# Loading the adjacency matrix through GpSimd's DMA path with a type conversion, in a graph layer with residual and layer norm

## The chip, the cores and the metric

One core of a Trainium2 chip. The metric is the time of one execution on the device in microseconds; lower is better. All inputs and the output lie in the chip's memory in float32, adj in int32.

## What is computed

x is 8 x 2048 x 512, adj is 2048 x 2048 of zeros and ones (int32), W is 512 x 1024.

```python
Wi, Wj = W[:, :512], W[:, 512:]
mi = einsum('bkd,od->bko', x, Wi)
mj = einsum('bkd,od->bko', x, Wj)
a = adj.astype(float32)
deg = a.sum(axis=1)
y = x + deg[None, :, None] * (mi + b) + einsum('ij,bjo->bio', a, mj)
out = (y - mean(y)) / sqrt(var(y) + 1e-5)      # over the last axis
```

The kernel receives x also as tiles transposed for TensorE (xt), and adj transposed and cut into 64 chunks: adjt[q, j] holds 128 rows j of the transposed matrix by 512 columns q, 256 KB in int32.

## The kernel before

**Stages.** The program runs batch 0, then a loop over batches 1 to 6, then batch 7. A batch has 16 tiles of 128 nodes. First the projections: for each tile n, TensorE makes mj and mi, each as a cross product (L343, 4 matmuls) and a main product (L351 and L353, 8 matmuls). Then the aggregations: for each tile i, 32 matmuls (L375) of the widened adjacency columns adjT with all of mj_hi and mj_lo of the batch. Numbers are split into a part of high bits and a rest so that TensorE's products keep float32 precision; hence x_top, x_hi, x_lo, x_df for x, and mj_hi, mj_lo for mj.

**Start.** Tiles 0 and 1 of batch 0 are projected straight from float32 weights (project_native), while VectorE and ScalarE split the 8 weight chunks (split_w L555 to L561, copy_w_hi L425). w_top, a scratch of that splitting, lies in the upper half of adjT8's columns.

**One projected tile, engine by engine.** Every engine has its own instruction stream, worked off in order, and waits on semaphores.
- VectorE (L665 to L681): mj(n) from PSUM (L587); the split of x(n+2) into x_top (L576) and the rest (L579), which waits for x_df(n+1), since x_top is one buffer (L575); mi(n) from PSUM (L594).
- ScalarE (L493 to L513): x_hi(n+1) and x_lo(n+1) (L443, L445), the copies of the cross products (L454), the load of x_raw(n+3), mj_hi(n) (L458).
- GpSimd (L300 to L307): x_df(n+1) (L281) after x_lo(n+1), then mj_lo(n) (L286) after mj_hi(n).
- TensorE (L380 to L392): the two halves of tile n, h = 0 after x_df(n) (L337).
- SP (L221 to L232): stores mi(n) to a buffer in the chip's memory.

**One aggregated tile.** ScalarE widens 128 columns of adjT8, from int8 to float32, into adjT (L470; two buffers). GpSimd adds the bias to mi read back (add_bias, L292). VectorE makes the residual with deg (L622), then, when TensorE is done, the sum and the layer norm (L628 to L649). agg_ps has two buffers.

**The adjacency, in batch 0 alone.** SP loads a chunk c as int32 into one of AB = 4 staging buffers adj_in (L176); ScalarE casts it to int8 into its place in adjT8 (cast_chunk, L465); VectorE adds the same int32 buffer into deg_part, the running sum of 16 chunks (count_chunk, L605 for the first of 16, L608 for the others). A buffer is loaded again when cast and count are both done (L174, L175). From deg_part TensorE makes the degrees (L360) once for each of four column blocks. Two lists written out by hand set the order, two chunks for each projected tile from tile 2 and up to four for each aggregated tile:

```python
PROJ_CHUNKS = [0, 0, 2, 2, 2, 2, 2, 2, 2, 2, 2, 2, 2, 2, 2, 2]
AGG_CHUNKS = [2, 3, 3, 3, 3, 3, 3, 4, 4, 4, 4, 0, 0, 0, 0, 0]
```

In a projected tile the first chunk is counted after the split of x(n+2), the second after mi(n). SP issues the loads of the chunks at matching places between its stores. The staging buffers 2 and 3 hold, before that, the first two tiles of x (x_first, L91).

Of the kernel before, what the change touches and what calls it, by code (L numbers as in the profile page):

```python
# [5 lines left out]
def bass_adj_resnorm(nc, x, xt, adjt, wt, b, out):  # L6
    fp32 = mybir.dt.float32
    fp32r = mybir.dt.float32r
    bf16 = mybir.dt.bfloat16
    i32 = mybir.dt.int32  # L10
    u32 = mybir.dt.uint32
    i8 = mybir.dt.int8
    ALU = mybir.AluOpType
# [8 lines left out]
    IB = N // DO  # L22
    TPB = DO // P
    GT = 4
    AB = 4
    NG = NT // GT
    NP = NT // 2
    TILES = NB * NT
# [11 lines left out]
    with ctx:  # L40
# [25 lines left out]
        mi = sb("mi", [P, DO], fp32)  # L66
        mi_in = [sb(f"mi_in{s}", [P, DO], fp32) for s in range(2)]
        r = [sb(f"r{s}", [P, D], fp32) for s in range(GT)]
        adj_in = [sb(f"adj_in{s}", [P, DO], i32) for s in range(AB)]
        deg_part = [sb(f"deg_part{s}", [P, DO], fp32r) for s in range(2)]  # L70
        bias = sb("bias", [P, DO], fp32)
        deg = sb("deg", [P, NT], fp32)
# [15 lines left out]
        w_stage = [r[0], r[1], r[2], r[3], mi_in[0], mi_in[1], x_top, mi]  # L88
        scratch = [adjT8[:, 2 * q:2 * q + 2, N // 2:N].bitcast(fp32) for q in range(NT // 2)]
        w_top = scratch  # L90
        x_first = [adj_in[2][:, :].bitcast(fp32), adj_in[3][:, :].bitcast(fp32)]  # L91

        def halves(ap):
            return ap.rearrange("p (a d) -> p a d", a=2)
# [21 lines left out]
        mi_loaded = [sem(f"mi_loaded{s}") for s in range(2)]  # L116
        r_loaded = [sem(f"r_loaded{s}") for s in range(GT)]
        adj_loaded = [sem(f"adj_loaded{s}") for s in range(AB)]
        adj_cast = sem("adj_cast")
        deg_part_ready = sem("deg_part_ready")  # L120
        deg_in_psum = sem("deg_in_psum")
        deg_ready = sem("deg_ready")
# [46 lines left out]

        @block.sync  # L170
        def _(sp):
            def load_chunk(c):
                if c >= AB:
                    sp.wait_ge(adj_cast, c - AB + 1)  # L174
                    sp.wait_ge(deg_part_ready, c - AB + 1)  # L175
                sp.dma_start(adj_in[c % AB][:, :], adjt[c // NT, c % NT]).then_inc(adj_loaded[c % AB], 16)  # L176

            def store_mi(n):
                sp.wait_ge(mi_ready, n + 1)
                sp.dma_start(mi_dram[n], mi[:, :]).then_inc(mi_stored, 16)  # L180

            sp.dma_start(x_first[0], xt[0]).then_inc(x_first_loaded[0], 16)
            for c in range(DK + 1, 2 * DK):
                sp.dma_start(w_stage[c][:, :], wt[c]).then_inc(w_loaded[c], 16)
            sp.dma_start(x_first[1], xt[1]).then_inc(x_first_loaded[1], 16)
            for c in range(DK):
                sp.dma_start(w_stage[c][:, :], wt[c]).then_inc(w_loaded[c], 16)
            for s in range(2):
                sp.dma_start(x_raw[s][:, :], xt[NATIVE + s]).then_inc(x_loaded[s], 16)
            sp.dma_start(bias[:, :], b.partition_broadcast(P)).then_inc(b_loaded, 16)  # L190
            for c in range(2):
                load_chunk(c)
            for n in range(NATIVE):
                sp.wait_ge(main_done, NATIVE + n + 1)
                load_chunk(2 + n)
                store_mi(n)

            def load_mi(m, u):
# [5 lines left out]
            def batch(bt):  # L204
                zero = known(bt) and bt == 0
                final = known(bt) and bt == NB - 1
                base = NT * bt

                def first_loads():
                    if zero:  # L210
                        sp.wait_ge(w_ready, 2 * DK)
                        sp.wait_ge(main_done, 2 * NATIVE)
                    sp.wait_ge(mi_stored, 16 * (base + 2))
                    for u in range(2):
                        load_mi(base + u, u)
                    for u in range(GT - 1):
                        if not zero:
                            sp.wait_ge(out_stored[u], 16 * NG * bt)
                        load_r(base + u, u)

                def proj(g):  # L221
                    for u in range(GT):
                        if zero and GT * g + u < NATIVE:
                            continue
                        if zero:
                            for c in proj_chunks(GT * g + u)[:-1]:
                                load_chunk(c + AB)
                        store_mi(base + GT * g + u)
                        if zero:
                            load_chunk(proj_chunks(GT * g + u)[-1] + AB)  # L230
                        if known(g) and g == NG - 1 and u == 1:
                            first_loads()  # L232

                over_groups(sp, zero, True, proj)

                def agg(g):
                    for u in range(GT):
                        i = GT * g + u
                        m = base + i
                        begin = known(g) and g == 0  # L240
                        ending = known(g) and g == NG - 1
                        if begin and u == 0:
                            sp.wait_ge(mi_stored, 16 * (base + NT))
                        if not (ending and u >= GT - 2):
                            sp.wait_ge(res_ready, m + 1)
                            load_mi(m + 2, u)
                        if not (ending and u >= 1):
                            if not (zero and begin and u == 0):
                                sp.wait_ge(out_stored[(u + 3) % GT], 16 * (NG * bt + g + (u + 3) // GT))
                            load_r(m + 3, (u + 3) % GT)  # L250
                        if zero:
                            for c in agg_chunks(i):
                                if c + AB < CHUNKS:
                                    load_chunk(c + AB)
                        sp.wait_ge(norm_ready, m + 1)
                        if final and ending and u == GT - 1:
                            sp.dma_start(out_tiles[m, :, 0:DO // 2], r[u][:, 0:DO // 2]).then_inc(out_stored[u], 16)
                        else:
                            sp.dma_start(out_tiles[m], r[u][:, :]).then_inc(out_stored[u], 16)

                agg(0)
                if zero:
                    for g in range(1, NG - 1):
                        agg(g)
                else:
                    with sp.Fori(1, NG - 1) as g:
                        agg(g)
                agg(NG - 1)
# [6 lines left out]
        def _(pool):  # L275
# [14 lines left out]
            def add_bias(m, u, turn):  # L290
                pool.wait_ge(mi_loaded[u % 2], turn)
                pool.tensor_tensor(mi_in[u % 2][:, :], mi_in[u % 2][:, :], bias[:, :], ALU.add).then_inc(mib_ready, 1)  # L292

            difference(NATIVE, 0)

            def batch(bt):
                zero = known(bt) and bt == 0
# [2 lines left out]
                def proj(g):  # L300
                    for u in range(GT):
# [3 lines left out]
                        if not (final and known(g) and g == NG - 1 and u == GT - 1):  # L305
                            difference(n + 1, (u + 1) % 2)
                        rest_of_mj(n, GT * g + u)  # L307

                over_groups(pool, zero, final, proj)
                if zero:  # L310
                    pool.wait_ge(b_loaded, 16)
                with pool.Fori(0, NP) as k:
                    for u in range(2):
                        add_bias(NT * bt + 2 * k + u, u, 16 * (NP * bt + k + 1))

            over_batches(pool, batch)

# [104 lines left out]
        def _(act):  # L422
# [35 lines left out]
                nc.scalar.activation(mj_hi[:, bass.ds(t, 1), :].rearrange("p t d -> p (t d)"), mj[:, :],  # L458
                                     ACT.Copy).then_inc(mj_hi_ready, 1)

            def cast_chunk(c):
                s = c % AB
                act.wait_ge(adj_loaded[s], 16 * (c // AB + 1))
                q, j = c // NT, c % NT
                nc.scalar.activation(adjT8[:, j, q * DO:(q + 1) * DO], adj_in[s][:, :], ACT.Copy).then_inc(adj_cast, 1)  # L465

            def widen(i, s, chunks):
                if chunks is not None:
                    act.wait_ge(adj_cast, chunks)
                nc.scalar.activation(adjT[s][:, :, :], adjT8[:, :, bass.ds(i * P, P)], ACT.Copy).then_inc(adjT_ready, 1)  # L470

            def root(m):
# [16 lines left out]
            def batch(bt):  # L489
# [3 lines left out]
                def proj(g):  # L493
                    last_group = known(g) and g == NG - 1
                    for u in range(GT):
# [6 lines left out]
                        take_cross(n, 0)  # L502
                        if not (final and last_group and u >= GT - 3):
                            load_x(n + 3, (u + 1) % 2)
                        if zero:
                            for c in proj_chunks(t)[:-1]:
                                cast_chunk(c)
                        take_cross(n, 1)
                        top_of_mj(n, t)
                        if zero:  # L510
                            cast_chunk(proj_chunks(t)[-1])
                        if last_group and u in (0, 2):
                            widen(u // 2, u // 2, NT if zero else None)  # L513

# [7 lines left out]
                    proj(NG - 1)  # L522
                if zero:
                    for i in range(NT):
                        for c in agg_chunks(i):
                            cast_chunk(c)
                        if i < NT - 2:
                            act.wait_ge(agg_done, i + 1)
                            widen(i + 2, i % 2, NT * ((i + 2) // TPB + 1))
                        if i == NT - 1:  # L530
                            parts(NT + 1, 1)
                        root(i)
# [18 lines left out]
        def _(dve):  # L551
# [43 lines left out]
                                               ALU.mult, ALU.subtract).then_inc(mi_ready, 1)  # L595

            def count_chunk(c):
                s = c % AB
                dve.wait_ge(adj_loaded[s], 16 * (c // AB + 1))
                q = c // NT  # L600
                part = deg_part[q % 2]
                if c % NT == 0:
                    if q >= 2:
                        dve.wait_ge(deg_in_psum, q - 1)
                    nc.vector.tensor_copy(part[:, :], adj_in[s][:, :]).then_inc(deg_part_ready, 1)  # L605
                else:
                    dve.wait_ge(deg_part_ready, c)
                    nc.vector.tensor_tensor(part[:, :], part[:, :].bitcast(fp32), adj_in[s][:, :],  # L608
                                            ALU.add).then_inc(deg_part_ready, 1)

            def take_degrees(q):
# [133 lines left out]
```

## Time and profile before

| | us |
|---|---|
| median of 3 runs | 1643.63 (1643.55 to 1643.64) |
| the profiled execution, whole | 1643.72 |
| its span | 1641.9 |
| TensorE busy | 1634.2 |
| VectorE busy | 844.8 |
| ScalarE busy | 661.7 |
| GpSimd busy | 498.4 |

The page gives the busy time of each engine (PE is TensorE's matmuls, PEld its weight loads, DVE is VectorE, ACT ScalarE, POOL GpSimd) and the chain that ended last, followed back from the end. The timeline gives start, duration and engine, and behind "<-" what ended an engine's idle time. TensorE's clock was granted at 0.999 of full speed.

### The profile page before, as it was taken

The numbers are of one execution on the slowest core, as the hardware profiler recorded it, in microseconds if no ns is written. First come the engines' busy times: TensorE is split into PE (matmuls) and PEld (weight loads), VectorE is DVE, ScalarE is ACT, GpSimd is POOL, SyncE is SP. The second block draws the span as 40 slices with busy tenths as digits, with TensorE's granted clock in tenths as the row PEclk, the third lists the DMA queues.
The fourth block names the chain that finished last, engine by engine and source line by source line (L and its number), as shares of the span: only waits on it lengthen the run. The fifth ranks groups of instructions, "written<-read, shape, count | busy, mean of one in ns | idle before, by whom it ended". The sixth has DMA issues, their size and how long they took to land.

```text
span 1641.9 us, 24654 instructions
## 1 busy us (share of the span) xinstructions
PE 1634.2 (100%) x7196; PEld 1346.8 (82%) x7196; DVE 844.8 (51%) x1879; ACT 661.7 (40%) x964; POOL 498.4 (30%) x386
## 2 busy tenths in 40 slices
PE   9999999999999999999999999999999999999998
PEld 6888888888888888888888888888888888888886
DVE  8787644554444544444544544444544454544544
ACT  5765445332453324532245332452325522255221
POOL 3532134311343114431144211442114421144210
PEclk9999999999999999999999999999999999999999
DMA  6676422332234323243223332233323333233332
GB/s 205 193 226 223 141 84 94 131 108 96 83 102 133 100 93 96 89 134 109 84 95 101 123 115 83 95 114 117 102 83 102 124 106 106 74 101 115 96 115 70
DMA packets 102843, 187.27 MB, mean 114 GB/s; under 512 B 11424, under 2 KB 11680, under 8 KB 102816
## 3 DMA queue, kind: packets, MB, share of 16 engines
q1 hardware_dynamic: 84672, 154.05, 29.1%
q10 hardware_dynamic: 18144, 32.91, 6.3%
q8 instruction: 11, 0.18, 0.0%
q14 instruction: 16, 0.13, 0.0%
HBM read 119.80 MB, written 67.11 MB: 114 GB/s over the span
## 4 chain that ended last, share of the span: by engine, by line
PE 98%; DVE 1%; DMA 0%; issue 0%; POOL 0%; ACT 0%; DVEq 0%
PE agg_ps L375 57%; PE cross_ps L343 14%; PE main_ps L351 14%; PE main_ps L353 14%; DVE W_lo L558 0%; DVE W_df L561 0%; DMA mi_in<-in_wt 0%; DVE adjT L555 0%; DVE x_raw L579 0%; DVE mj_lo L568 0%; PE deg_ps L360 0%; POOL x_df L281 0%; DVE x_top L576 0%; DVE stats L630 0%; DVE r L628 0%
## 5 line engine op out<-in xcount | busy, mean ns | idle before, releaser
L375 PE MATMUL agg_ps<-mj_hi,adjT 128*128 128x512 f32 x2048 | 797.0, 389 | 0.0
L375 PE MATMUL agg_ps<-mj_lo,adjT 128*128 128x512 f32 x2048 | 796.7, 389 | 0.0
L470 ACT ACTIVATE adjT<-adjT 128x2048 fp32r (+1 forms) x128 | 245.4, 1917 | 562.8 <-PE agg_ps L375 562.8
L375 PEld LDWEIGHTS agg_ps<-mj_hi,adjT 128*128 128x128 f32 x2048 | 384.5, 188 | 79.9
L375 PEld LDWEIGHTS agg_ps<-mj_lo,adjT 128*128 128x128 f32 x2048 | 384.3, 188 | 79.7
L351 PE MATMUL main_ps<-W_hi,x_hi 128*128 128x512 f32 x1008 | 392.3, 389 | 0.0
L353 PE MATMUL main_ps<-W_lo,x_lo 128*128 128x512 f32 x1008 | 392.1, 389 | 0.0
L292 POOL TENSOR_TENSOR mi_in<-mi_in,bias 128x512 f32<-128x512 f32 x128 | 166.9, 1307 | 649.9 <-DMA mi_in<-mi_dram 649.9
L628 DVE TENSOR_TENSOR r<-agg_ps,r 128x512 f32<-128x512 f32 x128 | 88.6, 692 | 355.0 <-PE agg_ps L375 354.9
L343 PE MATMUL cross_ps<-W_df,x_df 128*128 128x512 f32 x1008 | 270.2, 390 | 0.6 <-DVE W_df L561 0.5
L286 POOL TENSOR_TENSOR mj_lo<-mj,mj_hi 128x512 f32 (+1 forms) x126 | 166.7, 1323 | 323.4 <-ACT mj_hi L458 323.4
L454 ACT ACTIVATE cross<-cross_ps 128x512 f32<-128x512 f32 x252 | 148.6, 590 | 215.0 <-PE cross_ps L343 213.5
L343 PEld LDWEIGHTS cross_ps<-W_df,x_df 128*128 128x128 f32 x1008 | 189.0, 188 | 40.9 <-DVE W_df L561 0.9
L351 PEld LDWEIGHTS main_ps<-W_hi,x_hi 128*128 128x128 f32 x1008 | 189.3, 188 | 39.8 <-DVE mi L594 0.3
L353 PEld LDWEIGHTS main_ps<-W_lo,x_lo 128*128 128x128 f32 x1008 | 189.1, 188 | 39.2
L281 POOL TENSOR_TENSOR x_df<-x_top,x_lo 128x512 fp32r<-128x512 f32 x126 | 164.9, 1309 | 150.1 <-ACT x_lo L445 149.8
L587 DVE SCALAR_TENSOR_TENSOR mj<-main_ps,cross 128x512 f32<-128x512 f32 x126 | 87.1, 691 | 224.0 <-PE main_ps L353 218.8
L594 DVE SCALAR_TENSOR_TENSOR mi<-main_ps,cross 128x512 f32<-128x512 f32 x126 | 87.0, 691 | 107.6 <-PE main_ps L353 105.7
L622 DVE SCALAR_TENSOR_TENSOR r<-mi_in,deg,r 128x512 f32<-128x512 f32 x128 | 101.4, 796 | 13.1 <-POOL mi_in L292 9.2
L443 ACT ACTIVATE x_hi<-x_top 128x512 fp32r<-128x512 f32 x126 | 79.6, 632 | 63.3 <-PE main_ps L353 61.3
L630 DVE BATCH_NORM_STATS2 stats<-r 128x6 f32<-128x512 f32 x128 | 89.0, 695 | 11.7
L579 DVE TENSOR_TENSOR x_raw<-x_raw,x_top 128x512 f32<-128x512 f32 x126 | 87.3, 693 | 4.3
(59 smaller groups left out, 592.1 us busy)
## 6 DMA issues: line engine op xcount, KB each, us to landing
mi_dram<-mi SPq DMA_DIRECT2D x128, 256.0 KB, 2.1
mi_in<-mi_dram SPq DMA_DIRECT2D x128, 256.0 KB, 2.7
r<-in_x SPq DMA_DIRECT2D x128, 256.0 KB, 2.6
out<-r SPq DMA_DIRECT2D x127, 256.0 KB, 2.1
x_raw<-in_xt ACTq DMA_DIRECT2D x124, 256.0 KB, 2.7
adj_in<-in_adjt SPq DMA_DIRECT2D x64, 256.0 KB, 3.9
r<-in_wt SPq DMA_DIRECT2D x4, 256.0 KB, 5.2
adj_in<-in_xt SPq DMA_DIRECT2D x2, 256.0 KB, 4.0
```

The lines of the kernel that those rows point to most:

```text
L281: pool.tensor_tensor(x_df[s][:, :], x_top[:, :], x_lo[s][:, :].bitcast(fp32), ALU.subtract).then_inc(x_df_ready, 1)
L286: pool.tensor_tensor(mj_lo[:, bass.ds(t, 1), :].rearrange("p t d -> p (t d)"), mj[:, :], mj_hi[:, bass.ds(t, 1), :].rearrange("p t d -> p ...
L292: pool.tensor_tensor(mi_in[u % 2][:, :], mi_in[u % 2][:, :], bias[:, :], ALU.add).then_inc(mib_ready, 1)
L343: last = nc.tensor.matmul(cross_ps[h][:, :], x_df[s][:, k * P:(k + 1) * P], W_df[:, half * DK + k, :], start=(k == 0), stop=(k == DK - 1))
L351: nc.tensor.matmul(main_ps[h][:, :], x_hi[s][:, k * P:(k + 1) * P], W_hi[:, half * DK + k, :], start=(k == 0), stop=False)
L353: last = nc.tensor.matmul(main_ps[h][:, :], x_lo[s][:, k * P:(k + 1) * P], W_lo[:, half * DK + k, :], start=False, stop=(k == DK - 1))
L375: last = nc.tensor.matmul(agg_ps[s][:, :], adjT[s][:, j, :], part[:, j, :], start=(j == 0 and part is mj_hi), stop=(j == NT - 1 and part i ...
L454: nc.scalar.activation(cross[h][:, :], cross_ps[h][:, :], ACT.Copy).then_inc(cross_ready, 1)
L470: nc.scalar.activation(adjT[s][:, :, :], adjT8[:, :, bass.ds(i * P, P)], ACT.Copy).then_inc(adjT_ready, 1)
L622: nc.vector.scalar_tensor_tensor(r[u][:, :], mi_in[u % 2][:, :], deg[:, bass.ds(i, 1)], r[u][:, :], ALU.mult, ALU.add).then_inc(res_ready, 1)
L628: nc.vector.tensor_tensor(r[u][:, :], agg_ps[s][:, :], r[u][:, :], ALU.add).then_inc(sum_ready, 1)
L630: nc.vector.bn_stats(stats[:, :], r[u][:, :]).then_inc(ln_step, 1)
```

## The change

The chunks are loaded by GpSimd's DMA path, with int32 made int8 by the transfer, straight into adjT8. The casts on ScalarE and the staging buffers go; counting reads adjT8's int8. The number of chunks in flight, AB, goes from 4 to 8; a chunk c is issued when count c - 8 is done. Chunks 0 and 1 are issued before x_df of tile 2, chunks 2 to 7 directly behind it. In batch 0's projections chunks c + 8 follow mj_lo(n) in GpSimd's stream; in its aggregation they follow add_bias of the next tile, in a loop now written out. Chunk 32 also waits for the weights to be split. x_first gets two buffers of its own.

```diff
-    AB = 4
+    AB = 8
-        adj_in = [sb(f"adj_in{s}", [P, DO], i32) for s in range(AB)]
+        x_first = [sb(f"x_first{s}", [P, D], fp32) for s in range(2)]
...
         @block.sync
-            def load_chunk(c):
-                if c >= AB:
-                    sp.wait_ge(adj_cast, c - AB + 1)
-                    sp.wait_ge(deg_part_ready, c - AB + 1)
-                sp.dma_start(adj_in[c % AB][:, :], adjt[c // NT, c % NT]).then_inc(adj_loaded[c % AB], 16)
...
-            for c in range(2):
-                load_chunk(c)
             for n in range(NATIVE):
-                sp.wait_ge(main_done, NATIVE + n + 1)
-                load_chunk(2 + n)
                 store_mi(n)
...
         @block.gpsimd
+            def load_chunk(c):
+                q, j = c // NT, c % NT
+                if c >= AB:
+                    pool.wait_ge(deg_part_ready, c - AB + 1)
+                if q == 2 and j == 0:
+                    pool.wait_ge(w_ready, 2 * DK)
+                    pool.wait_ge(w_hi_ready, 2 * DK)
+                pool.dma_start(adjT8[:, j, q * DO:(q + 1) * DO], adjt[q, j]).then_inc(adj_loaded[c % AB], 16)
+
+            for c in range(2):
+                load_chunk(c)
             difference(NATIVE, 0)
+            for c in range(2, AB):
+                load_chunk(c)
...
                         rest_of_mj(n, GT * g + u)
+                        if zero:
+                            for c in proj_chunks(GT * g + u):
+                                load_chunk(c + AB)
...
+                if zero:
+                    for i in range(NT):
+                        add_bias(i, i % 2, 16 * (i // 2 + 1))
+                        if i:
+                            for c in agg_chunks(i - 1):
+                                if c + AB < CHUNKS:
+                                    load_chunk(c + AB)
...
         @block.scalar
-            def cast_chunk(c):
-                s = c % AB
-                act.wait_ge(adj_loaded[s], 16 * (c // AB + 1))
-                q, j = c // NT, c % NT
-                nc.scalar.activation(adjT8[:, j, q * DO:(q + 1) * DO], adj_in[s][:, :], ACT.Copy).then_inc(adj_cast, 1)
-
             def widen(i, s, chunks):
                 if chunks is not None:
-                    act.wait_ge(adj_cast, chunks)
+                    act.wait_ge(deg_part_ready, chunks)
...
         @block.vector
             def count_chunk(c):
-                s = c % AB
-                dve.wait_ge(adj_loaded[s], 16 * (c // AB + 1))
-                q = c // NT
-                part = deg_part[q % 2]
-                if c % NT == 0:
+                dve.wait_ge(adj_loaded[c % AB], 16 * (c // AB + 1))
+                q, j = c // NT, c % NT
+                part, chunk = deg_part[q % 2], adjT8[:, j, q * DO:(q + 1) * DO]
+                if j == 0:
                     if q >= 2:
                         dve.wait_ge(deg_in_psum, q - 1)
-                    nc.vector.tensor_copy(part[:, :], adj_in[s][:, :]).then_inc(deg_part_ready, 1)
+                    nc.vector.tensor_copy(part[:, :], chunk).then_inc(deg_part_ready, 1)
                 else:
                     dve.wait_ge(deg_part_ready, c)
-                    nc.vector.tensor_tensor(part[:, :], part[:, :].bitcast(fp32), adj_in[s][:, :],
+                    nc.vector.tensor_tensor(part[:, :], part[:, :].bitcast(fp32), chunk,
                                             ALU.add).then_inc(deg_part_ready, 1)
```

The calls of load_chunk on SP and of cast_chunk on ScalarE in batch 0's tiles go too.

## Rows read from the trace of the kernel before

**Rows 1.** The page: busy time and share of the span; chain that ended last.

```profile
PE 1634.2 (100%) x7196; PEld 1346.8 (82%) x7196; DVE 844.8 (51%) x1879; ACT 661.7 (40%) x964; POOL 498.4 (30%) x386
PE 98%; DVE 1%; DMA 0%; issue 0%; POOL 0%; ACT 0%; DVEq 0%
```

**Rows 2.** Busy time by stretch, the projections of batch 0; then clock, DMA share, GB/s.

```profile
25.00:97.00 72.00, 72.00 (x319) 59.45 (x320) 57.37 (x82) 54.14 (x96) 38.42 (x27) 1.00 0.65 200
```

**Rows 3.** Timeline, TensorE: tiles 3, 4 and 15, and aggregation (start us, us).

```profile
24.95 1.20 PE L343 MATMUL cross_ps<-W_df,x_df 128*128 128x512 f32 x4
30.52 1.07 PE L343 MATMUL cross_ps<-W_df,x_df 128*128 128x512 f32 x4
...
91.02 1.07 PE L343 MATMUL cross_ps<-W_df,x_df 128*128 128x512 f32 x4
96.46 0.39 PE L375 MATMUL agg_ps<-mj_hi,adjT 128*128 128x512 f32 x1
```

**Rows 4.** Groups of instructions, 0 to 160 us, ScalarE's casts of the chunks.

```profile
L465 ACT ACTIVATE adjT<-adj_in 128x512 int8<-128x512 int32 x55 | 33.8, 625 | 6.8 <-DMA adj_in<-in_adjt 6.7
```

**Rows 5.** Timeline: an issue on SP, and GpSimd's instruction at its longest.

```profile
17.15 0.34 SPq L180 DMA_DIRECT2D mi_dram<-mi  x1
...
46.57 1.75 POOL L286 TENSOR_TENSOR mj_lo<-mj,mj_hi 128x512 fp32r<-128x512 f32 x1 [2.22 <-ACT mj_hi L458]
```

**Rows 6.** Timeline, the start: first weight, VectorE's start, GpSimd's gap and VectorE's instruction in it.

```profile
0.75 0.42 ACTq L476 DMA_DIRECT2D mi_in<-in_wt  x1
4.15 0.43 DVE L555 TENSOR_SCALAR adjT<-mi_in 128x512 uint32<-128x512 uint32 x1 [4.15 <-DMA mi_in<-in_wt]
16.20 1.45 POOL L281 TENSOR_TENSOR x_df<-x_top,x_lo 128x512 fp32r<-128x512 f32 x1 [15.21 <-ACT x_lo L445]
18.12 0.42 DVE L555 TENSOR_SCALAR adjT<-r 128x512 uint32<-128x512 uint32 x1
23.60 1.29 POOL L281 TENSOR_TENSOR x_df<-x_top,x_lo 128x512 fp32r<-128x512 f32 x1 [5.95 <-ACT x_lo L445]
```

**Rows 7.** DMA: GB/s in 40 slices of 0 to 220 us; KB and us to landing.

```profile
GB/s 204 399 121 182 95 192 194 194 237 199 219 201 202 172 180 122 275 339 207 161 252 238 214 203 216 219 206 240 243 225 235 279 77 143 103 97 43 48 49 95
...
adj_in<-in_adjt SPq DMA_DIRECT2D x64, 256.0 KB, 3.9
```

**Rows 8.** Timeline, GpSimd and VectorE: split, count, mi and count of projected tiles.

```profile
51.91 0.69 DVE L608 TENSOR_TENSOR deg_part<-deg_part,adj_in 128x512 fp32r<-128x512 f32 x1
52.63 0.69 DVE L594 SCALAR_TENSOR_TENSOR mi<-main_ps,cross 128x512 f32<-128x512 f32 x1
53.24 1.06 DVE L608 TENSOR_TENSOR deg_part<-deg_part,adj_in 128x512 fp32r<-128x512 f32 x1
...
93.96 1.30 POOL L281 TENSOR_TENSOR x_df<-x_top,x_lo 128x512 fp32r<-128x512 f32 x1 [2.00 <-ACT x_lo L445]
95.39 0.43 DVE L576 TENSOR_SCALAR x_top<-x_raw 128x512 uint32<-128x512 uint32 x1 [0.24 <-POOL x_df L281]
95.85 0.69 DVE L579 TENSOR_TENSOR x_raw<-x_raw,x_top 128x512 f32<-128x512 f32 x1
96.46 1.78 DVE L608 TENSOR_TENSOR deg_part<-deg_part,adj_in 128x512 fp32r<-128x512 f32 x1
```

**Rows 9.** Timeline, GpSimd and VectorE: the first chunks counted, beside an x_df.

```profile
26.10 1.52 DVE L605 CAST deg_part<-adj_in 128x512 fp32r<-128x512 int32 x1
27.30 1.47 POOL L281 TENSOR_TENSOR x_df<-x_top,x_lo 128x512 fp32r<-128x512 f32 x1
28.14 1.18 DVE L608 TENSOR_TENSOR deg_part<-deg_part,adj_in 128x512 fp32r<-128x512 f32 x1
```

**Rows 10.** Timeline, aggregation of batch 0: idle before add_bias and the sum; four counts.

```profile
140.34 1.30 POOL L292 TENSOR_TENSOR mi_in<-mi_in,bias 128x512 f32<-128x512 f32 x1 [6.04 <-DMA mi_in<-mi_dram]
140.75 0.69 DVE L628 TENSOR_TENSOR r<-agg_ps,r 128x512 f32<-128x512 f32 x1 [0.80 <-PE agg_ps L375]
159.27 3.08 DVE L608 TENSOR_TENSOR deg_part<-deg_part,adj_in 128x512 fp32r<-128x512 f32 x4
```

More of the change, by code:

```diff
@@ L9, in bass_adj_resnorm @@
     bf16 = mybir.dt.bfloat16
-    i32 = mybir.dt.int32
     u32 = mybir.dt.uint32
@@ L90, in bass_adj_resnorm @@
         w_top = scratch
-        x_first = [adj_in[2][:, :].bitcast(fp32), adj_in[3][:, :].bitcast(fp32)]
         def halves(ap):
@@ L118, in bass_adj_resnorm @@
         adj_loaded = [sem(f"adj_loaded{s}") for s in range(AB)]
-        adj_cast = sem("adj_cast")
         deg_part_ready = sem("deg_part_ready")
@@ L180, in store_mi @@
                 sp.dma_start(mi_dram[n], mi[:, :]).then_inc(mi_stored, 16)
-            sp.dma_start(x_first[0], xt[0]).then_inc(x_first_loaded[0], 16)
+            sp.dma_start(x_first[0][:, :], xt[0]).then_inc(x_first_loaded[0], 16)
             for c in range(DK + 1, 2 * DK):
                 sp.dma_start(w_stage[c][:, :], wt[c]).then_inc(w_loaded[c], 16)
-            sp.dma_start(x_first[1], xt[1]).then_inc(x_first_loaded[1], 16)
+            sp.dma_start(x_first[1][:, :], xt[1]).then_inc(x_first_loaded[1], 16)
             for c in range(DK):
@@ L224, in proj @@
                             continue
-                        if zero:
-                            for c in proj_chunks(GT * g + u)[:-1]:
-                                load_chunk(c + AB)
                         store_mi(base + GT * g + u)
-                        if zero:
-                            load_chunk(proj_chunks(GT * g + u)[-1] + AB)
                         if known(g) and g == NG - 1 and u == 1:
@@ L250, in agg @@
                             load_r(m + 3, (u + 3) % GT)
[L251 to L254, printed above, removed]
                         sp.wait_ge(norm_ready, m + 1)
@@ L311, in batch @@
                     pool.wait_ge(b_loaded, 16)
-                with pool.Fori(0, NP) as k:
-                    for u in range(2):
-                        add_bias(NT * bt + 2 * k + u, u, 16 * (NP * bt + k + 1))
+                if zero:
[5 more added lines that the diff above has]
+                                    load_chunk(c + AB)
+                else:
+                    with pool.Fori(0, NP) as k:
+                        for u in range(2):
+                            add_bias(NT * bt + 2 * k + u, u, 16 * (NP * bt + k + 1))
             over_batches(pool, batch)
@@ L504, in proj @@
                             load_x(n + 3, (u + 1) % 2)
-                        if zero:
-                            for c in proj_chunks(t)[:-1]:
-                                cast_chunk(c)
                         take_cross(n, 1)
                         top_of_mj(n, t)
-                        if zero:
-                            cast_chunk(proj_chunks(t)[-1])
                         if last_group and u in (0, 2):
@@ L524, in batch @@
                     for i in range(NT):
-                        for c in agg_chunks(i):
-                            cast_chunk(c)
                         if i < NT - 2:
```

## The prediction

> **What bounds the kernel now.** I read the page's busy shares and chain first. TensorE is busy for 1634.2 of 1641.9 us and carries 98% of the chain [rows 1]. So a change to the loading of adj can gain next to nothing; what it can do is make TensorE wait, and only in batch 0, where adj is loaded. I then read the stretches: in the projections of batch 0 (25 to 97 us) TensorE is busy throughout, but VectorE works 57 of 72 us, ScalarE 54, GpSimd 38 [rows 2]. GpSimd has the most room by that row; the question is whether it has room at the right moment. The starts of TensorE's tiles give the pace: tile 3 starts at 24.95, tile 4 at 30.52, tile 15 at 91.02, and aggregation at 96.46 [rows 3]. A tile takes 5.44 us (93.74 is its second half, 2.72 later and 2.72 before 96.46). Tile 3 starts 0.06 us after its x_df ends (23.60 + 1.29), so TensorE waits for x_df as soon as that is late.
>
> **What is removed.** 64 casts on ScalarE of 0.63 us [rows 4], and 64 loads on SP. ScalarE is not waited for by TensorE in the projections, so this gains nothing there. TensorE's 13 tiles 3 to 15 take 96.46 - 24.95 = 71.51 us where 13 times 5.44 is 70.72: at most 0.8 us could come back, part of it degree matmuls. I take 0. SP loses work that hid behind its waits, and its stores of mi come no later: 0. The staging buffers cost no time.
>
> **What is added: the issue on GpSimd.** Call I the time for which GpSimd is held by one converting load. The trace has no load from GpSimd. Its lower bound is an issue on SP, 0.34 us, or the first on ScalarE's queue, 0.42 [rows 5, 6]; the upper bound is the longest of GpSimd's own 512-column instructions, 1.75 us [rows 5]. GpSimd builds the transfer by its own program, as it does its elementwise work, but has only 128 rows to describe, not 512 columns to compute. I take the middle, 1.0 us, and keep both ends. The Trainium skill, "DMA: Bandwidth & Descriptors", section Specifications, gives about 1 us to the first byte on GpSimd's path and 0.6 on SP's; by these the sum would be that of I = 1.0. No row here shows it.
>
> **Start.** Two loads go out from GpSimd while the first weights travel. The first weight chunk is issued at 0.75 and releases VectorE at 4.15, which then works without a gap of note until x_df of tile 3 [rows 6]. Two chunks of 262 KB at the 399 GB/s that the next slice reaches cost 0.66 us each [rows 7]; most of them fall behind the first weight. Bounds 0 and 0.66, I take 0.3. Then six loads in a row (chunks 2 to 7) stand behind x_df of tile 2. GpSimd is free from 16.20 + 1.45 = 17.65 and next starts x_df of tile 3 at 23.60, 5.95 us later [rows 6]. Six loads at 1.0 take 6.0: 0.05 us late. VectorE runs three x_top or w_top instructions in that gap (0.42 us each, one shown); if each holds GpSimd off, 1.26 us more. Bounds 0 and 1.26, I take 0.6. Together 0.65, all on TensorE's path, since tile 3 waits for that x_df.
>
> **The loop.** This is the large term. In the new order GpSimd does, per tile n: x_df(n+1), mj_lo(n), load a (waits for VectorE's first count), load b (waits for its last count, which stands behind mi(n)). Only then comes x_df(n+2). VectorE in turn holds the split of x(n+3) until x_df(n+2) is done, because x_top is one buffer, and its two counts and mi(n+1) stand behind that split. That closes a ring that the old order did not have, since GpSimd never waited for a count. Its length, from the end X of an x_df, by [rows 8]: x_top starts X+0.13 (95.26 to 95.39), the subtraction 0.46 later at X+0.59. GpSimd's mj_lo, now behind the loads and with its input long ready, runs from X to X+1.30. The rows show what two such instructions do together: a count that began at 28.14, inside GpSimd's 27.30 to 28.77, ended at 29.32, 0.55 after it [rows 9], against 0.69 undisturbed. So the subtraction ends at X+1.85, the count of a starts 0.08 before that and ends at X+2.46; mi starts 0.72 after the count's start, X+2.49; the last count 0.61 later, X+3.10, to X+3.79. A wait across engines takes 0.07, so load b is issued at X+3.86 and ends at X+3.86+I. Load a (from X+2.53) is over by then if I is under 1.33. x_df takes 1.30. A turn is 5.16 + I, which I round to 5.15 + I: 6.15 us at I = 1.0, against TensorE's 5.44. Counting from int8 is costed as before: the count is 512 columns either way, 0.69 undisturbed.
>
> First turn: x_df(3) ends 24.89 as now. The first count, a cast, ends at 27.62 [rows 9]. Load a 27.7 to 28.7. The next count, no longer beside an x_df, takes 0.69 from 28.14, to 28.83; load b 28.9 to 29.9; x_df(4) ends 31.2. Eleven turns of 6.15 are 67.65: x_df(15) ends at 98.85, tile 15 starts at 98.9 against 91.02: 7.9 us. In general 12 I - 4.1: the small slack that there is now is in the 4.1. Tile 15 then runs into aggregation as before.
>
> **Aggregation: 0.** Up to four loads stand behind an add_bias. GpSimd idles 6.04 us before one, and VectorE waits 0.80 us for TensorE in a tile with three counts; with four (3.08 us) it has no gap, but agg_ps is double [rows 10]. Four loads of 1.0 and 1.30 for add_bias fit in the 7.25 of a tile. If that cover were gone, each microsecond over would be lost once per tile, over eleven tiles. Landing: 3.9 us now [rows 7], while a chunk is asked for eight counts, four tiles, before its use. Batches 1 to 7 have the same instructions.
>
> **Sum.** 7.9 + 0.65 + 0.3 = 8.85 us. The profiled execution took 1643.72 (span 1641.9): 1652.6; the median of the runs is 0.1 below it: **1652.5 us**. About 0.2%, 3.3 us, is what can be told from no change here.
>
> **Rivals.**
> 1. The ring as above, I from 0.75 to 1.2: 12 x 0.75 - 4.1 = 4.9 to 12 x 1.2 - 4.1 = 10.3, with 1.25 + 0.6 + 0.6 at the start 12.8: 1648.5 to 1656.4. Chance 0.56.
> 2. **Not slower: the issue is cheap.** GpSimd hands a load on as SP does. At 0.42 us the ring turns in 5.57, and the loss is 12 x 0.42 - 4.1 = 0.9, with 0.3 at the start 1644.8. It decides below I = 0.59, where 12 I - 4.1 + 0.3 is 3.3. For it: SP's row. Against it: GpSimd is slower than VectorE at the same 512 columns, 1.30 against 0.69. Chance 0.15.
> 3. **Ports.** The rows show a VectorE instruction with two SBUF inputs and a GpSimd one excluding each other. If that holds for a load too, load a (X+2.53) is drawn out by the last count's 0.69 and ends at X+4.22, load b at X+5.22, and a turn is 6.52: 12 x 0.36 = 4.3 us more, 1656.8. Against it: a load reads no tensor on GpSimd. Chance 0.12. The Trainium skill, "SBUF — State Buffer", section Who interferes with whom, says that it is VectorE's two-port instructions that keep GpSimd from writing descriptors, and that two SBUF inputs do not. By that rule load b meets only mj (PSUM input), this rival falls, and only the burst at the start, which meets x_top and w_top, is drawn out, which leaves 1652.5. No row here has a load on GpSimd to agree or not.
> 4. **GpSimd itself is the bound.** Over 1.33 the turn is 3.83 + 2 I. At 1.5: x_df(4) at 32.0, eleven turns of 6.83, tile 15 late by 16.2, burst 3.05 + 0.6, start 0.3: 20.1, 1663.8; at 1.75 some 28.7. Chance 0.12.
> 5. **Converting makes landing slow**, and the counts wait. It needs more than 20 us where 3.9 is seen; at 30 us a ring of eight gives a tile per 7.5, some 29 us over 14 tiles, and more in aggregation. Chance 0.03. That something I cannot name makes it faster: 0.02; with 0.8 us to get, not by 0.2%.
>
> **Numbers.** The likeliest is case 1, 1652.5, with 1648.5 to 1656.4 as its own range. Taking in rival 3 and the upper part of 2: 1646 to 1660. Left out are most of 2, 4 and 5. Slower by over 0.2%: 0.56 + 0.12 + 0.12 + 0.03 = 0.83; within: 0.15; faster: 0.02.
>
> **What would show it.** Chain of waits, 28 to 100 us: TensorE's cross_ps waiting for x_df, about 0.7 us per tile; x_df of batch 0 spaced 6.1 and not 5.44; aggregation starting near 105, not 96.46; from there every later stretch as long as before. GpSimd's load instructions give I directly: 0.4 would make it rival 2, 1.5 rival 4. No idle of VectorE before a count for a landing. If TensorE waits in aggregation, or tile 3 starts over 2 us late, my zero or my start is wrong. If x_df is spaced 6.1 but TensorE waits for something else, the ring is not the one I named.

## The result, and the profile after

The changed kernel takes **1652.57 us** (median of 4 runs, 1652.36 to 1654.26) against 1643.61 before: 9.0 us slower, ratio 1.0056 with an interval of 1.0044 to 1.0068. The forecast was 1652.5. The profiled execution took 1652.49, its span is 1650.4 against 1641.9. So 8.5 us of the loss lie within the span; the whole execution is 2.1 us longer than its span, against 1.8 before, and no trace shows what these 0.3 us are (runs 4 and 5 below have 1.8 again).

The page of the changed kernel, busy time and chain:

```profile
PE 1636.9 (99%) x7196; PEld 1345.6 (82%) x7196; DVE 847.0 (51%) x1879; ACT 628.5 (38%) x900; POOL 527.9 (32%) x450
...
q0 software_dynamic: 9216, 4.20, 3.5%
...
PE 94%; DVE 3%; POOL 1%; issue 1%; ACT 0%; DMA 0%; DVEq 0%
```

Against [rows 1], ScalarE has lost 33 us of work and GpSimd has gained 30; the 64 loads appear as a queue of their own, q0. The chain now runs through VectorE and GpSimd for 4% of the span, which is the new wait. Where it is, the starts of TensorE's tiles show (timeline, TensorE: tiles 3, 4, 5, 8, 9, 15 and the first matmul of aggregation; start us, us):

```profile
25.20 1.14 PE L345 MATMUL cross_ps<-W_df,x_df 128*128 128x512 f32 x4
31.20 1.20 PE L345 MATMUL cross_ps<-W_df,x_df 128*128 128x512 f32 x4 [0.30 <-POOL x_df L259]
37.53 1.20 PE L345 MATMUL cross_ps<-W_df,x_df 128*128 128x512 f32 x4 [0.54 <-POOL x_df L259]
...
56.15 1.19 PE L345 MATMUL cross_ps<-W_df,x_df 128*128 128x512 f32 x4 [0.47 <-POOL x_df L259]
62.36 1.19 PE L345 MATMUL cross_ps<-W_df,x_df 128*128 128x512 f32 x4 [0.47 <-POOL x_df L259]
...
99.32 1.19 PE L345 MATMUL cross_ps<-W_df,x_df 128*128 128x512 f32 x4 [0.42 <-POOL x_df L259]
...
104.89 0.39 PE L377 MATMUL agg_ps<-mj_hi,adjT 128*128 128x512 f32 x1
```

Tile 3 is 0.25 us later than in [rows 3], tile 4 0.68, tile 15 8.30, aggregation 8.43, and the span ends 8.5 later. Nearly all is lost between tiles 3 and 15, where a tile takes 6.20 us and not 5.44, and each waits for x_df. One turn on GpSimd and VectorE (timeline, in order of time within each engine; compare [rows 8]):

```profile
42.39 1.29 POOL L259 TENSOR_TENSOR x_df<-x_top,x_lo 128x512 fp32r<-128x512 f32 x1
43.63 1.29 POOL L264 TENSOR_TENSOR mj_lo<-mj,mj_hi 128x512 fp32r<-128x512 f32 x1
46.85 0.57 POOL L279 DMA_DIRECT2D adjT<-in_adjt  x1 [1.92 <-DVE deg_part L596]
48.05 0.53 POOL L279 DMA_DIRECT2D adjT<-in_adjt  x1 [0.64 <-DVE deg_part L596]
48.59 1.30 POOL L259 TENSOR_TENSOR x_df<-x_top,x_lo 128x512 fp32r<-128x512 f32 x1
...
43.82 1.40 DVE L565 TENSOR_SCALAR x_top<-x_raw 128x512 uint32<-128x512 uint32 x1 [1.67 <-POOL x_df L259]
45.25 0.69 DVE L568 TENSOR_TENSOR x_raw<-x_raw,x_top 128x512 f32<-128x512 f32 x1
45.86 0.68 DVE L596 TENSOR_TENSOR deg_part<-deg_part,adjT 128x512 fp32r<-128x512 f32 x1
46.47 0.69 DVE L583 SCALAR_TENSOR_TENSOR mi<-main_ps,cross 128x512 f32<-128x512 f32 x1
47.07 0.68 DVE L596 TENSOR_TENSOR deg_part<-deg_part,adjT 128x512 fp32r<-128x512 f32 x1
```

Follow one turn, from x_df to x_df: x_df ends at 43.68, x_top starts 0.14 later but needs 1.40 us, because mj_lo (43.63 to 44.92) holds it off; the split, two counts and mi follow without a gap until 47.75; the last load is recorded from 48.05 to 48.58; x_df starts at 48.59. So a load takes 0.84 us of the ring, 0.30 before its record and 0.54 in it. From the end of x_df to the end of the last count are 4.07 us (43.68 to 47.75), and the turn is 4.07 + 0.84 + 1.30 = 6.21.

At the start (timeline; compare [rows 6]):

```profile
4.35 0.43 DVE L544 TENSOR_SCALAR adjT<-mi_in 128x512 uint32<-128x512 uint32 x1 [4.35 <-DMA mi_in<-in_wt]
17.79 3.38 POOL L279 DMA_DIRECT2D adjT<-in_adjt  x6
23.79 1.29 POOL L259 TENSOR_TENSOR x_df<-x_top,x_lo 128x512 fp32r<-128x512 f32 x1 [2.62 <-ACT x_lo L447]
```

The first weight lands 0.20 us later. The burst of six loads takes 3.38 us, and GpSimd still idles 2.62 before x_df of tile 3.

### The profile page after: what moved, and what is told of

Its sections match the earlier page's. It is cut to its first block, busy times and chain, and to the rows that moved or that the text cites. A ratio compares the mean times of both kernels' runs of the same rounds, so it can differ in the third digit from the quotient of the medians.

```text
span 1650.4 us, 24507 instructions
## 1 busy us (share of the span) xinstructions
PE 1636.9 (99%) x7196; PEld 1345.6 (82%) x7196; DVE 847.0 (51%) x1879; ACT 628.5 (38%) x900; POOL 527.9 (32%) x450
## 3 DMA queue, kind: packets, MB, share of 16 engines
q1 hardware_dynamic: 75456, 137.27, 25.9%
## 4 chain that ended last, share of the span: by engine, by line
PE 94%; DVE 3%; POOL 1%; issue 1%; ACT 0%; DMA 0%; DVEq 0%
PE agg_ps L377 56%; PE cross_ps L345 12%; PE main_ps L355 12%; PE main_ps L353 12%; POOL x_df L259 1%; DVE x_top L565 1%; DVE x_raw L568 1%; DVE deg_part L596 0%; POOL adjT L279 0%; ACT cross L456 0%; DVE W_lo L547 0%; DVE W_df L550 0%; DMA mi_in<-in_wt 0%; DVE adjT L544 0%; DVE deg_part L593 0%
```

## The experiments

Three theories for the 9 us. The ring: count, load, x_df, split of x, count. Occupancy: GpSimd has too much to do with two loads per tile. Landing or conversion: the counts wait for slow transfers. Ratios are against the kernel before, run beside each group: 1643.63 for runs 1 to 4, 1643.74 for runs 5 to 8.

**1. Twelve slots, loads at the same places.** Here a slot is only a semaphore, as the chunks go straight to adjT8.

```diff
-    AB = 8
+    AB = 12
+    AHEAD = 8
...
-                                load_chunk(c + AB)
+                                load_chunk(c + AHEAD)
```

Expected: 

> Twelve slots in place of eight, loads issued at the same places of GpSimd's stream and as many: a load now waits for a count two tiles older, long done. Ring theory (count, load, x_df, split of x, count): the ring is cut, x_df spaced 5.44 us, 8.3 us of the 8.9 come back, some 0.3 us of the start stays: 1643.9. Occupancy theory (GpSimd simply has too much to do with two loads per tile): unchanged, 1652.5. Landing theory (the counts wait for slow transfers): a little better at most, 1651 to 1652.

Measured: 1648.29 us (8 runs), ratio 1.0029 (1.0018 to 1.0040). None of the three times that were expected. The waits before the loads are gone, and with the same two loads about half of the loss came back, so occupancy of GpSimd is not the cause. But a tile takes 5.73, not 5.44. VectorE is busy 70.26 of the 72 us from 25 to 97. One tile (timeline):

```profile
55.03 1.47 POOL L265 TENSOR_TENSOR mj_lo<-mj,mj_hi 128x512 fp32r<-128x512 f32 x1 [1.91 <-ACT mj_hi L461]
56.44 1.10 POOL L280 DMA_DIRECT2D adjT<-in_adjt  x2
57.55 1.31 POOL L260 TENSOR_TENSOR x_df<-x_top,x_lo 128x512 fp32r<-128x512 f32 x1
...
55.26 1.79 DVE L597 TENSOR_TENSOR deg_part<-deg_part,adjT 128x512 fp32r<-128x512 f32 x1
56.97 0.68 DVE L584 SCALAR_TENSOR_TENSOR mi<-main_ps,cross 128x512 f32<-128x512 f32 x1
57.57 1.85 DVE L597 TENSOR_TENSOR deg_part<-deg_part,adjT 128x512 fp32r<-128x512 f32 x1
```

The two loads push x_df behind them to where it starts just ahead of the last count (57.55 against 57.57). That count then takes 1.85 us, and the first one, beside mj_lo, 1.79, where 0.69 is undisturbed. VectorE has no gap left and sets the pace; TensorE waits for mi (L584). Cutting the ring uncovered a second limit that the place of the loads creates. It is not all of the rest: in this trace tile 3 starts at 25.64, 0.7 us late, aggregation at 99.30, 2.8 late, and the span ends 4.1 late, so another 1.3 us go in aggregation, where TensorE waits for deg_part ahead of the degrees.

**2. Loads one tile later in GpSimd's stream**, eight slots.

```diff
                             difference(n + 1, (u + 1) % 2)
-                        rest_of_mj(n, GT * g + u)
                         if zero:
-                            for c in proj_chunks(GT * g + u):
+                            for c in proj_chunks(GT * g + u - 1):
+                                load_chunk(c + AB)
+                        rest_of_mj(n, GT * g + u)
+                        if zero and GT * g + u == NT - 1:
+                            for c in proj_chunks(NT - 1):
                                 load_chunk(c + AB)
```

Expected: 

> Eight slots as in the change, but the two loads of tile n-1 are issued between x_df(n+1) and mj_lo(n), one tile later. Ring theory: the counts waited for are done, the ring is cut, 1643.9 as with twelve slots. Occupancy theory: the same instructions on GpSimd, 1652.5. Landing theory: loads go out later, so 1652.5 or more.

Measured: 1644.52 us (10 runs, 1643.90 to 1647.18), ratio 1.0007 (0.9998 to 1.0017). As the ring theory says, and x_df keeps its early place, so the second limit stays away too. TensorE is busy for 72.00 of the 72 us from 25 to 97. GpSimd there, and one x_top of VectorE (timeline):

```profile
43.05 1.29 POOL L259 TENSOR_TENSOR x_df<-x_top,x_lo 128x512 fp32r<-128x512 f32 x1 [0.61 <-ACT x_lo L450]
44.28 0.57 POOL L279 DMA_DIRECT2D adjT<-in_adjt  x1
45.19 0.75 POOL L279 DMA_DIRECT2D adjT<-in_adjt  x1 [0.34 <-DVE deg_part L599]
46.58 1.72 POOL L264 TENSOR_TENSOR mj_lo<-mj,mj_hi 128x512 fp32r<-128x512 f32 x1 [0.65 <-ACT mj_hi L463]
48.49 1.51 POOL L259 TENSOR_TENSOR x_df<-x_top,x_lo 128x512 fp32r<-128x512 f32 x1 [0.19 <-ACT x_lo L450]
...
45.41 0.41 DVE L568 TENSOR_SCALAR x_top<-x_raw 128x512 uint32<-128x512 uint32 x1
```

The second load still waits for a count, 0.34 us, but x_df is ahead of it. What stands behind the wait, mj_lo and the next x_df, is not held up by it: GpSimd is through with the load and then idles 0.65 and 0.19 us for their inputs from ScalarE. The second load is longer than the first, 0.75 against 0.57 us; run 5 comes back to that.

**3. Both counts ahead of mi.**

```diff
-                            for c in proj_chunks(t)[:-1]:
+                            for c in proj_chunks(t):
                                 count_chunk(c)
                         combine_mi(n)
-                        if zero:
-                            count_chunk(proj_chunks(t)[-1])
```

Expected: 

> VectorE counts both chunks of a tile before mi(n) and not around it. Ring theory: mi's 0.60 us leaves the ring, a turn goes from 6.20 to about 5.60 us, eleven turns give 6.6 back: 1645.5 to 1646.5. Occupancy and landing theories: the same loads on GpSimd and the same transfers, 1652.5.

Measured: 1649.60 us (5 runs), ratio 1.0039 (1.0024 to 1.0053). In the right direction and less than said. x_df is spaced 5.82 (47.03 to 52.85), not 5.60:

```profile
51.50 0.57 POOL L279 DMA_DIRECT2D adjT<-in_adjt  x1 [1.92 <-DVE deg_part L596]
52.30 0.53 POOL L279 DMA_DIRECT2D adjT<-in_adjt  x1 [0.23 <-issue]
52.85 1.30 POOL L259 TENSOR_TENSOR x_df<-x_top,x_lo 128x512 fp32r<-128x512 f32 x1
```

The last count now ends before the second load can begin, so both loads stand in the ring, one behind the other with 0.23 between them (52.07 to 52.30). I had left load a out of the ring, and with mi moved it is in it. Also mi is now the late one: TensorE waits for it (17 to 220 us: 6.4 us ahead of weight loads, 2.1 ahead of matmuls) and no longer for x_df, but for one wait of 0.3.

**4. The issue moved, without the conversion.** The kernel before with int32 staging in six buffers and casts on ScalarE; only the issue goes to GpSimd, at the change's places.

```diff
-    AB = 4
+    AB = 6
...
         @block.gpsimd
+            def load_chunk(c):
+                if c >= AB:
+                    pool.wait_ge(adj_cast, c - AB + 1)
+                    pool.wait_ge(deg_part_ready, c - AB + 1)
...
+                pool.dma_start(adj_in[c % AB][:, :], adjt[c // NT, c % NT]).then_inc(adj_loaded[c % AB], 16)
```

Expected: 

> The kernel before, with int32 staging and casts on ScalarE, but the chunks issued by GpSimd at the places of the change, six staging buffers. Ring theory: where the loads stand in GpSimd's stream is what costs, not the conversion: a turn of 6.2, loss 7 to 9 us, 1651 to 1653. Conversion theory (slow converting transfers, or int8 counting): 1643.6 to 1645.

Measured: 1655.19 us (4 runs), ratio 1.0073 (1.0056 to 1.0089). The loss is there without any conversion and with counts from int32, so these are not its cause. It is larger by 2.6 us than the change's: a turn is 6.47, x_df starting at 49.48 and 55.95. The last count of such a turn ends at 61.29 (60.61 + 0.68), but the load's record starts at 61.86:

```profile
60.65 0.56 POOL L281 DMA_DIRECT2D adj_in<-in_adjt  x1 [2.18 <-DVE deg_part L612]
61.86 0.54 POOL L281 DMA_DIRECT2D adj_in<-in_adjt  x1 [0.65 <-DVE deg_part L612]
...
60.61 0.68 DVE L612 TENSOR_TENSOR deg_part<-deg_part,adj_in 128x512 fp32r<-128x512 f32 x1
```

That is 0.57 us where the change has 0.30. The difference between the two is a second wait ahead of the load, on the cast, which was over by 61.21. That it is the number of waits was not tried by itself.

**5. Two issues for each chunk**, of 256 columns each.

```diff
-                pool.dma_start(adjT8[:, j, q * DO:(q + 1) * DO], adjt[q, j]).then_inc(adj_loaded[c % AB], 16)
+                for h in range(2):
+                    lo = h * (DO // 2)
+                    pool.dma_start(adjT8[:, j, q * DO + lo:q * DO + lo + DO // 2],
+                                   adjt[q, j, :, lo:lo + DO // 2]).then_inc(adj_loaded[c % AB], 16)
...
-                dve.wait_ge(adj_loaded[c % AB], 16 * (c // AB + 1))
+                dve.wait_ge(adj_loaded[c % AB], 32 * (c // AB + 1))
```

Expected: 

> Each chunk is loaded as two halves of 256 columns, so two issues in place of one, the same bytes. Ring theory: only load b stands in the ring; it grows by the 0.55 us that an issue was seen to hold GpSimd, a turn goes from 6.20 to 6.75, eleven turns cost 6.0 more; the burst at the start goes from 3.4 to 6.8 us and is 0.8 late: 1659 to 1660. Landing theory: the same bytes, 1652.5. If the issue's cost were a fixed wait and not the issue, also 1652.5.

Measured: 1659.84 us (4 runs), ratio 1.0098 (1.0081 to 1.0115), as the ring theory said: x_df is spaced 6.71 (51.91 to 58.62), in three of twelve turns 7.0 to 7.1, and why in these is open. With the same bytes 7.3 us more: what counts is the issue. The rows of the start also show what VectorE's instructions do to an issue (timeline: the twelve loads in one row, two of them by themselves, four loads of a later turn; then VectorE):

```profile
18.23 6.76 POOL L281 DMA_DIRECT2D adjT<-in_adjt  x12
20.36 0.72 POOL L281 DMA_DIRECT2D adjT<-in_adjt  x1
22.10 0.77 POOL L281 DMA_DIRECT2D adjT<-in_adjt  x1
...
56.36 2.26 POOL L281 DMA_DIRECT2D adjT<-in_adjt  x4 [1.92 <-DVE deg_part L599]
...
18.75 0.41 DVE L547 TENSOR_SCALAR adjT<-r 128x512 uint32<-128x512 uint32 x1
20.53 0.42 DVE L547 TENSOR_SCALAR adjT<-r 128x512 uint32<-128x512 uint32 x1
22.32 0.42 DVE L568 TENSOR_SCALAR x_top<-x_raw 128x512 uint32<-128x512 uint32 x1
```

The twelve loads take 6.76 / 12 = 0.563 us on average, but they are not alike. Two take 0.72 and 0.77 us, the others 0.55 to 0.58. In the two long ones a w_top or x_top starts 0.17 and 0.22 us after the load, and the load ends 0.13 us after that instruction (20.95 and 21.08; 22.74 and 22.87). The w_top of 18.75, which begins 0.05 us ahead of its load, costs nothing. Four loads beside mi, a count and mj take 2.26 / 4 = 0.565: these do not draw a load out. Run 2 has both sides. The load at 45.19 meets an x_top 0.22 us after its start and takes 0.75; where x_top starts 0.24 after, it is x_top that takes 0.55 in place of 0.42 (timeline of run 2):

```profile
55.72 0.54 POOL L279 DMA_DIRECT2D adjT<-in_adjt  x1
55.96 0.55 DVE L568 TENSOR_SCALAR x_top<-x_raw 128x512 uint32<-128x512 uint32 x1
```

In runs 2, 7 and 8 all twelve x_top that start 0.24 to 0.25 us into a load take 0.54 to 0.55, and their loads 0.54. So a load and an x_top or w_top exclude each other for a part of the load, and where they meet one of them is 0.1 to 0.2 us longer. The Trainium skill, "SBUF — State Buffer", section Who interferes with whom, says that a two-port instruction of VectorE blocks descriptor writing on GpSimd. For x_top and w_top these rows agree, at 0.2 us for a load that is held.

**6. mj_lo cut short.** This kernel leaves out part of the computation: mj_lo of batch 0's tiles 2 to 14 is computed for 16 of 512 columns, the rest is zero.

```diff
+            pool.memset(mj_lo[:, NATIVE:NT - 1, :].bitcast(fp32), 0.0).then_inc(zeroed, 1)
+            pool.wait_ge(zeroed, 3)
...
+                if known(n) and n < NT - 1:
+                    pool.tensor_tensor(mj_lo[:, n, 0:16], mj[:, 0:16], mj_hi[:, n, 0:16].bitcast(fp32),
+                                       ALU.subtract).then_inc(mj_lo_ready, 1)
+                    return
```

Expected: 

> Left out: the rest mj_lo of batch 0's tiles 2 to 14, but for 16 of 512 columns (the others are set to zero at the start). mj_lo does not stand in the ring; what it could do is hold x_top off, 1.40 us where 0.42 is undisturbed. Ring with port lock: the turn falls by 0.98 to 5.22, under the 5.44 of TensorE, and the time to 1644 to 1644.5. Ring without port lock (x_top slow for another reason): turn 6.20, 1652.5.

Measured: 1646.33 us (10 runs), ratio 1.0018 (1.0008 to 1.0027). The tiles from 30 to 70 us are spaced 5.44, TensorE's own pace, so an instruction that is not in the ring lengthened it. x_top is back at its length:

```profile
57.66 1.31 POOL L261 TENSOR_TENSOR x_df<-x_top,x_lo 128x512 fp32r<-128x512 f32 x1
59.54 0.22 POOL L267 TENSOR_TENSOR mj_lo<-mj,mj_hi 128x16 fp32r<-128x16 f32 x1 [0.58 <-ACT mj_hi L466]
...
59.10 0.43 DVE L571 TENSOR_SCALAR x_top<-x_raw 128x512 uint32<-128x512 uint32 x1 [0.97 <-POOL x_df L261]
```

Of the 2.6 us that remain, 2.2 are there when tile 3 starts. They came from the added memset, in the same way, seen at the start (timeline, GpSimd and VectorE):

```profile
0.92 5.64 POOL L256 MEMSET mj_lo<- 128x6656 f32 x1
4.14 2.71 DVE L550 TENSOR_SCALAR adjT<-mi_in 128x512 uint32<-128x512 uint32 x1 [4.14 <-DMA mi_in<-in_wt]
```

VectorE's first instruction takes 2.71 us and ends 0.29 after the memset; tile 3 starts 2.24 later than before, at 27.19. I had not allowed for that in the time expected, and the run missed it by 1.8 us.

**7. As 2, and chunks 0 and 1 issued behind x_df of tile 2.**

```diff
-            for c in range(2):
-                load_chunk(c)
             difference(NATIVE, 0)
-            for c in range(2, AB):
+            for c in range(AB):
                 load_chunk(c)
```

Expected: 

> The order of the run with the loads one tile later, and also chunks 0 and 1 issued behind x_df of tile 2 instead of during the weights. If these two cost the start its 0.2 us by bandwidth, tile 3 starts at 24.95 again and the time is 1643.6 to 1644.0, with a spread as small as that of the kernel before; if the spread of 1643.9 to 1647.2 stays, it comes from elsewhere on GpSimd's path.

Measured: 1643.96 us (10 runs, 1643.63 to 1645.24), ratio 1.0002 (0.9992 to 1.0012). The first weight is there at 3.93, tile 3 starts at 24.69. This is the best form with the change's loading, and no different from the kernel before. From run 2 it is not clearly apart either, by the two intervals. The spread is smaller than in 2 but larger than that of the kernel before (1643.33 to 1644.48); where the rest of it comes from is open.

**8. As 2, with twelve slots.**

```diff
-    AB = 8
+    AB = 12
+    AHEAD = 8
...
-                                load_chunk(c + AB)
+                                load_chunk(c + AHEAD)
```

Expected: 

> Loads one tile later in GpSimd's stream and twelve slots. Twelve slots at the old places left a turn of 5.73 us, with VectorE full because x_df, pushed behind the two loads, met its last count. Port theory of that remainder: the place matters, not the slots, so this gives 1644 to 1644.5. If the remainder came from the twelve slots (more transfers in flight), 1648.

Measured: 1645.32 us (10 runs), ratio 1.0011 (1.0002 to 1.0021): near 2 and far from the 1648.29 of 1, so it is the place that made the second limit. Its tiles from 30 to 66 us are spaced 5.44. In its trace tile 3 starts at 25.82, 0.7 later than in 2, and the lateness against the kernel before grows from 0.6 us at the start of aggregation to 1.3 at the end of the span: TensorE waits for deg_part, longest ahead of the last block of degrees (178.46). One thing that delays VectorE shows: add_bias meets its layer norm, and an instruction of a single column takes 1.17 us (166.51, beside add_bias at 166.38) where it takes 0.16 undisturbed. Whether the slots cause either of the two was not tried; it is no gain at any rate.

## Why the prediction was right

**What bounds the kernel and the casts' worth** held: 33 us less work on ScalarE brought nothing.

**The ring** was the cause, at the place named: runs 2, 7 and 8 undo it by the order alone, run 5 lengthens it by an issue, run 4 has it without conversion. The turn was said to be 6.15 and is 6.20; x_df(4) was said to end at 31.2 and ends at 31.15; tile 15 was said to be late by 7.9 plus the start's 0.95 and is late by 8.30. **But this fit is in part luck: two errors that cancel.** The issue was taken as 1.0 us and 0.07 for the wait; it takes 0.84 with the wait. The formula 12 I - 4.1 with I = 0.77 would have given 5.1 us. What made up for it is x_top. I had let it run at X+0.13 in 0.42 us and the subtraction be held off by mj_lo, ending at X+1.85. In fact x_top was held off first, to X+1.54, and the subtraction ended at X+2.26; the last count ends at X+4.07 and not at X+3.79. Per turn the counts end 0.28 later than said and the load costs 0.23 less, so the sum came out. Run 6 shows what hangs on it. Without the 0.98 us for which mj_lo holds x_top off, the turn would be 6.21 - 0.98 = 5.23 us by my estimate, under TensorE's 5.44, and there the tiles are spaced 5.44: by these numbers the ring alone, without mj_lo beside it, would have cost nothing in the loop. The price of 0.07 for a wait that the prediction used for a load was too small as well, 0.30 up to the load's record.

**The burst** was said to cost 0.65 and cost 0: six loads took 3.38 us, not 6.0 to 7.3, inside a gap of 5.95. That VectorE's w_top and x_top hold GpSimd off there, which I had at up to 1.26 us, is real but small: one of the six loads takes 0.72 us (at 19.92, beside a w_top at 20.10). **The first weight** was said to cost 0.3 and costs 0.20. **Outside the span** I had nothing, and 0.3 us came there. **Aggregation** cost 0 as said: up to four loads stand behind add_bias, VectorE waits 0.80 us for TensorE as before, and the lateness goes from 8.43 at its start to 8.5 at the end of the span.

**The rivals.** The cheap issue: cheaper than I took it, but at 0.84 not at SP's 0.34, and with x_top's wait not cheap enough. Ports: in the form that I gave it (a count draws out a load) it fell, load a takes 0.57 beside a count; in others it is real. GpSimd's elementwise work holds off VectorE's x_top and counts, which makes the second limit of run 1, and x_top and w_top draw out a load by 0.2 us (run 5), but no load of the change's turns meets one. GpSimd as the bound: it idles in every turn (1.92 + 0.64 us). Its price at 1.75 us was also summed wrongly: 22.2 for tile 15, 4.55 + 0.6 for the burst and 0.3 make 27.6, not 28.7. Landing: 4.3 us against 3.9, 3.4 to 4.1 in the other runs that convert, and no count waits for it.

Open, beside the spread and the 0.3 us outside the span: I did not measure the 0.30 us between a count and the load's record apart from the load.

## What to carry to other kernels

Moving a transfer to another engine's queue moves its waits too. Before placing a load behind a "buffer free" wait in an in-order stream, list what stands behind it and follow whether that, through the other engines, feeds the very instruction waited for; compare that ring's length with the pace of the bounding engine, since an engine's low busy share does not show it. If the ring is there, shift the wait by one iteration: here a change of order gave back 8.1 of 9.0 us. That the two first loads, moved off the start, gave another half is not clear of the spread. And when a VectorE instruction stretches, look at what GpSimd does in the same microsecond. A row of several loads hides the long ones in its mean: look at them one by one.

## What the runs showed that I had not expected

- One x_top instruction (128x512, SBUF to SBUF, 0.42 us alone) took 1.40 us beside GpSimd's mj_lo, and a w_top of the same form 2.71 us beside a GpSimd memset, each ending 0.29 to 0.30 us after GpSimd's instruction. VectorE is held for the rest of that instruction.
- A load issued from GpSimd held that engine for 0.53 to 0.58 us in most cases, whether it moved 512 or 256 columns, with or without conversion. It took 0.71 to 0.77 us where an x_top or w_top started 0.17 to 0.23 us after it, and the first load of each program took 0.68 to 0.70.
- The transfers occupy the DMA engines somewhat longer converted than not. Queue q0's 3.5% of 1650.4 us is 57.8 us for 64 chunks, 0.90 us each, though it writes a quarter of the bytes; in run 4, from the same queue without conversion, 3.0% of 1653.4 us is 0.78 each. The queue that had them before went from 29.1% of 1641.9 us to 25.9% of 1650.4, by 50.3 us, 0.79 each. The shares are rounded to 0.1%, which is 0.03 us a chunk, and over the runs with 64 converting loads q0's lies between 3.5 and 3.8%.
